# An attention tower with experts on one core: score masks and row maxima cut into 32x32 tiles, and keys, values and value projections laid out in lots of 32 rows

## The reference

```python
Q, K, V = x @ wq, x @ wk, x @ wv            # 16 heads of 16
# local attention: query i sees the keys i-63 .. i
sc = Q_block @ [K_previous_block, K_own_block].T / 4     # 64 queries x 128 keys
sc = where((j > i) & (j <= i + 64) & (first block: j >= 64), sc, -inf)
local = softmax(sc) @ [V_previous_block, V_own_block]
# remote attention: 8 heads over 64 pooled latents, causal mask lmask
rem = softmax(where(lmask, GQ @ GK.T / 4, -inf)) @ GV @ r_out_w
out = (sigmoid(Q.gate_local) * local + sigmoid(Q.gate_remote) * rem) @ w_out
```

## Time and profile before

| what | value |
|---|---|
| median of 3 runs | 3002.09 us (2997.6 to 3002.82) |
| profiled execution | 3003.33 us |
| its span in the trace | 3001.5 us |
| PE matmul busy | 2668.5 us, 89% |
| PE weight loads busy | 1793.9 us, 60% |
| DVE busy | 1795.5 us, 60% |
| ACT busy | 1091.1 us, 36% |
| mean granted PE clock | 0.971 |

### The profile page before, as it was taken

One profiled execution on the slowest core, in us unless ns is written; L12 is line 12 of the kernel. 1 busy time (PEld: TensorE's weight loads), 2 busy tenths in 40 slices (PEclk: granted clock), 3 DMA queues, 4 the chain that ended last, 5 costly groups with the idle time before them and its releaser, 6 DMA issues. The chain is left out here.

```text
span 3001.5 us, 83138 instructions
## 1 busy us (share of the span) xinstructions
PE 2668.5 (89%) x32904; PEld 1793.9 (60%) x32904; DVE 1795.5 (60%) x5503; ACT 1091.1 (36%) x1898; POOL 752.9 (25%) x998
## 2 busy tenths in 40 slices
PE   2899899899999899899899994299999999999998
PEld 1566666666666566566666663166656565666666
DVE  4556556556556556566566556775767667675720
ACT  0343343343343343433333431143333434343343
POOL 1011111121121121121121100134444453434543
PEclk9999999999999999999999998599999999999999
DMA  2000000010010010010000001001020211101020
GB/s 71 11 23 24 17 24 23 17 28 18 17 28 18 18 29 16 19 28 16 21 26 16 23 9 45 15 29 59 30 64 28 65 46 49 64 28 61 30 67 29
DMA packets 51568, 93.71 MB, mean 31 GB/s; under 512 B 7980, under 2 KB 36728, under 8 KB 51096
## 3 DMA queue, kind: packets, MB, share of 16 engines
q0 software_dynamic: 18432, 50.36, 5.9%
q1 hardware_dynamic: 32792, 38.52, 3.9%
HBM read 55.29 MB, written 33.55 MB: 30 GB/s over the span
## 5 line engine op out<-in xcount | busy, mean ns | idle before, releaser
L985 PE MATMUL S_ps<-hT,w 128*128 128x512 f32 x1024 | 478.4, 614 | 15.1 <-ACT hT L694 12.1
L998 PE MATMUL O_ps<-w,hid 128*128 128x256 f32 x2048 | 460.3, 379 | 0.0
L496 POOL DMA_INDIRECT rows<-in_tok_table,idx_now x128 | 129.4, 1011 | 1171.5 <-PE M_ps L883 928.0
L998 PEld LDWEIGHTS O_ps<-w,hid 128*128 128x128 f32 x2048 | 383.0, 190 | 62.5 <-issue 15.3
L1096 DVE TENSOR_REDUCE mxL<-S_ps 128x16 f32<-128x2048 f32 x128 | 293.0, 2289 | 155.8 <-PE S_ps L804 155.8
L632 ACT ACTIVATE PT<-S_ps 128x2048 f32<-128x2048 f32 x128 | 240.3, 1878 | 279.0 <-PE S_ps L772 279.0
L705 ACT ACTIVATE hid<-S_ps,b 128x512 f32<-128x512 f32 x256 | 175.3, 687 | 425.4 <-PE S_ps L985 408.5
L985 PEld LDWEIGHTS S_ps<-hT,w 128*128 128x128 f32 x1024 | 190.0, 194 | 223.5 <-issue 212.1
L828 PEld LDWEIGHTS O_ps<-bdV,PT 128*64 128x64 f32 x7680 | 249.2, 138 | 53.4 <-issue 47.5
L665 ACT ACTIVATE bdV<-M_ps 64x256 f32<-64x256 f32 x256 | 98.8, 386 | 490.7 <-PE M_ps L900 489.2
L828 PE MATMUL O_ps<-bdV,PT 128*64 128x34 f32 x7680 | 263.6, 225 | 1.9 <-DVE loc L1112 1.9
(11 more groups left out here) (237 smaller groups left out, 4248.5 us busy)
## 6 DMA issues: line engine op xcount, KB each, us to landing
h_rows<-h SPq DMA_DIRECT2D x64, 256.0 KB, 2.1
w<-in_w SPq DMA_DIRECT2D x16, 1024.0 KB, 5.9
rows<-in_tok_table,idx_now POOLq DMA_INDIRECT x128, 3.5
out_rows<-orow,idx_cur POOLq DMA_INDIRECT x128, 2.4
PT<-in_tables SPq DMA_DIRECT2D x1, 1024.0 KB
b<-in_b SPq DMA_DIRECT2D x8, 128.0 KB, 4.9
hrow<-h_rows,idx_next POOLq DMA_INDIRECT x64
hrow<-h_rows,idx_cur POOLq DMA_INDIRECT x64
```

The source lines that it names most:

```text
L985: mm = nc.tensor.matmul(S_ps[:, m % 2, 0:GT * P], w1[:, c, m * P:(m + 1) * P], hT[g % 2][:, c, :], start=c == 0, stop=c == KC - 1)
L998: mm = nc.tensor.matmul(O_ps[:, q % 2, 0:D], hid[:, m, q * P:(q + 1) * P], w2[:, m, :], start=m == 0, stop=m == FC - 1)
```

## The change

Everything that was cut at 64 is cut at 32. `pe_masks` issues 16 matmuls in tiles of 32x32 in place of 8 in 64x64; row group n of the array always writes bank n, so the mask tables are stored in as many turned copies as needed (`latm` and `reach` four, `lreach` two, `band` three variants). An S6 item takes 96 keys for every 32 queries in place of 128 for 64: 32 fp32 matmuls of 192 moving columns in tiles of 32x32, in place of 16 of 256 in 32x64; the mask is 384 columns wide, and DVE reduces 1536 columns in place of 2048. `Kt` and `bdV` hold even and odd heads in alternating lots of 32 rows. The item V issues 16 matmuls of 128 columns and 8 of 40 in tiles of 128x32, in place of 8 in 128x64; ACT copies V with 128 partitions and a parity scale (`c_parity`, two columns more) in place of 64 partitions without one. The tables grow from 2048 to 3488 columns.

```diff
+QW = 32
+KW = W + QW
 ...
-    cols = [f(ident), f(parity), f(own), f(i), f(band), f(lat), f(np.roll(lat, W, 0)), f(before), f(lane), f(reach), f(lreach), f(pick)]
+    cols = [f(ident), f(parity), f(own), f(i), f(band), f(turned(lat, NG)), f(before), f(lane), f(turned(reach, NG)), f(turned(lreach, 2)), f(pick)]
 ...
-        Kt = [sba(f"Kt{j}", [P, KC, 1 + NB, 2, W]) for j in range(2)]
+        Kt = [sba(f"Kt{j}", [P, KC, 2 * (1 + NB), 2, QW]) for j in range(2)]
 ...
+                v = bank[:, 0:D].rearrange("p (a q d) -> p a q d", a=2, d=HD)
                 for j in range(2):
-                    v = bank[W * j:W * (j + 1), 0:D + 2 * (GW + E)].rearrange("p (a n) -> p a n", a=2)[:, :, 0:D // 2]
-                    nc.scalar.activation(bdV[par][W * j:W * (j + 1), 2 * k:2 * k + 2, :, j, 0:HD],
-                                         v.rearrange("p a (q d) -> p a q d", d=HD), ACT.Copy)
+                    nc.scalar.activation(bdV[par][:, 2 * k:2 * k + 2, :, j, 0:HD], v, ACT.Copy, scale=c_parity[:, 2 + j:3 + j])
 ...
         def pe_masks(pe, into, mask):
-            for g in range(0, NG, 2):
-                for a, n, rows_ in ((0, g, 0), (1, g, W), (1, g + 1, 0), (0, g + 1, W)):
-                    nc.tensor.matmul(into(S_ps[W * a:W * (a + 1), n, :]), identb[rows_:rows_ + W, rows_:rows_ + W],
-                                     mask(a, rows_), start=True, stop=False)
+            for n in range(NG):
+                own_ = slice(QW * n, QW * (n + 1))
+                for a in range(NG):
+                    nc.tensor.matmul(into(S_ps[QW * a:QW * (a + 1), n, :]), identb[own_, own_], mask(own_, a, (n - a) % NG),
+                                     start=True, stop=False)
 ...
-                        for a in range(2):
-                            x = 2 * t + a
-                            into = S_ps[W * a:W * (a + 1), g, D * c:D * (c + 1)].rearrange("p (j a k) -> p a j k", j=2, a=2)
-                            mm = nc.tensor.matmul(into, Qt[par][32 * g:32 * g + 32, c, W * x:W * (x + 1)],
-                                                  Kt[par][32 * g:32 * g + 32, c, x:x + 2, :, :], start=False, stop=c == KC - 1)
+                        for a in range(NG):
+                            x = NG * t + a
+                            into = S_ps[QW * a:QW * (a + 1), g, 2 * KW * c:2 * KW * (c + 1)].rearrange("p (j a k) -> p j a k", j=2, k=QW)
+                            mm = nc.tensor.matmul(into, Qt[par][32 * g:32 * g + 32, c, QW * x:QW * (x + 1)],
+                                                  Kt[par][32 * g:32 * g + 32, c, x:x + 3, :, :].rearrange("p a j k -> p j a k"),
+                                                  start=False, stop=c == KC - 1)
 ...
-                for n in range(2):
-                    lhs = [x1T[:, c, W * (2 * k + n):W * (2 * k + n + 1)] for c in range(KC)]
-                    to = n * (D // 2 + gates_)
+                lot = lambda c, n: x1T[:, c, P * k + QW * n:P * k + QW * (n + 1)]
+                for n in range(2):
                     for c in range(KC):
-                        for a, (lo, hi) in enumerate((even, odd)):
 ...
+                        for a in range(NG):
+                            mm = nc.tensor.matmul(bank[QW * a:QW * (a + 1), n * (D // 2):(n + 1) * (D // 2)], lot(c, 2 * n + a // 2),
+                                                  wvg[:, c, slice(*halves[a % 2])], start=c == 0, stop=c == KC - 1)
+                for c in range(KC):
+                    for a in range(NG):
+                        mm = nc.tensor.matmul(bank[QW * a:QW * (a + 1), D:D + GW + E], lot(c, a), wvg[:, c, gates_],
+                                              start=c == 0, stop=c == KC - 1)
 ...
-                    nc.vector.tensor_reduce(mxL[:, k - 6, :], S_ps[:, :, :].rearrange("p g (h n) -> p (g h) n", n=P),
+                    nc.vector.tensor_reduce(mxL[:, k - 6, :].rearrange("p (g h) -> p g h", g=NG),
+                                            S_ps[:, :, 0:4 * KW].rearrange("p g (h n) -> p g h n", n=KW),
                                             AX.X, ALU.max, negate=True).then_inc(s_mx, 1)
```

More of the change, by code:

```diff
@@ L58, in constants @@
     ident = np.eye(P, dtype=np.float32)
[L59 to L62, removed]
+    near, wide = i[:, None] % QW, np.arange(KW)[None, :]
+    ring = (wide > near) & (wide <= near + W)
+    band = np.stack([np.where(m, 0.0, NEG) for m in (ring & (wide >= W), ring & (wide >= W - QW), ring)], 1)
     tiles = S // P
@@ L65, in constants @@
     lat = np.where(np.arange(NL)[None, None, :] <= tok // (S // NL), 0.0, NEG)
-    parity = np.stack([(i // HD) % 2 == 0, (i // HD) % 2 == 1], 1)
+    parity = np.stack([(i // n) % 2 == j for n in (HD, QW) for j in range(2)], 1)
     own = (i[:, None] // HD == np.arange(LH)[None, :]) * (NL / S)
@@ L221, in tower @@
         mp = sba("mp", [P, TS, P])
-        reach = sba("reach", [P, 2 * W], BF16)
-        lreach = sba("lreach", [P, S], BF16)
+        reach = sba("reach", [P, NG, 2 * W], BF16)
+        lreach = sba("lreach", [P, 2, S], BF16)
         pick = sba("pick", [P, KC + 1, 2 * W], BF16)
@@ L240, in tower @@
         xf, xw, xs = (stage[0:SEQS, 6144 + S * n:6144 + S * (n + 1)] for n in (1, 2, 3))
[L241 to L242 removed]
+        woutT = stage[:, 3584:3584 + KC * D].rearrange("p (c n) -> p c n", c=KC)
+        ones = stage[:, 6144 + S:6144 + S + P]
         wvs = PL[:, 0, :].rearrange("p (c n) -> p c n", c=KC)
@@ L888, in pe_item @@
             elif name == "V":
-                even, odd, gates_ = (0, D // 2), (D // 2 + GW + E, D + GW + E), GW + E
+                halves, gates_ = ((0, D // 2), (D // 2 + GW + E, D + GW + E)), slice(D // 2, D // 2 + GW + E)
+                lot = lambda c, n: x1T[:, c, P * k + QW * n:P * k + QW * (n + 1)]
                 for n in range(2):
-                    lhs = [x1T[:, c, W * (2 * k + n):W * (2 * k + n + 1)] for c in range(KC)]
-                    to = n * (D // 2 + gates_)
                     for c in range(KC):
-                        for a, (lo, hi) in enumerate((even, odd)):
-                            first = to
-                            if a == n:
-                                lo, hi = (lo, hi + gates_) if a == 0 else (lo - gates_, hi)
-                                first = to if a == 0 else to - gates_
-                            mm = nc.tensor.matmul(bank[W * a:W * (a + 1), first:first + hi - lo], lhs[c], wvg[:, c, lo:hi],
-                                                  start=c == 0, stop=c == KC - 1)
+                        for a in range(NG):
+                            mm = nc.tensor.matmul(bank[QW * a:QW * (a + 1), n * (D // 2):(n + 1) * (D // 2)], lot(c, 2 * n + a // 2),
+                                                  wvg[:, c, slice(*halves[a % 2])], start=c == 0, stop=c == KC - 1)
+                for c in range(KC):
+                    for a in range(NG):
+                        mm = nc.tensor.matmul(bank[QW * a:QW * (a + 1), D:D + GW + E], lot(c, a), wvg[:, c, gates_],
+                                              start=c == 0, stop=c == KC - 1)
             mm.then_inc(s_misc, 1)
@@ L1361, in _ @@
             for par in range(2):
-                nc.vector.memset(Kt[par][:, :, 0, :, :], 0.0)
+                nc.vector.memset(Kt[par][:, :, 0:2, :, :], 0.0)
                 chain(dve, nc.vector.memset(bdV[par][:, :, :, :, :], 0.0))
-                nc.vector.memset(bdV[par][0:W, :, :, 0, HD:OW], 1.0)
-                nc.vector.memset(bdV[par][W:P, :, :, 1, HD:OW], 1.0)
+                for a in range(NG):
+                    nc.vector.memset(bdV[par][QW * a:QW * (a + 1), :, :, a % 2, HD:OW], 1.0)
                 chain(dve, nc.vector.memset(bdL[par][:, :, :, :], 0.0))
```

46 lines of the change are left out of this document (24 added, 22 removed).

## The result

The changed kernel takes 3023.16 us, median of 4 runs (3017.86 to 3026.01), beside 3002.45 us for the kernel before (its profiled execution counted in, four runs): a ratio of 1.0069, 95% interval 1.0049 to 1.0089. It is slower by about 21 us, where 87 us less had been forecast. The profiled execution is the fastest of the four, with a span of 3016.1 us.

The account below looks back on a forecast made before the run. PE was taken to bound the kernel. Per sequence 1.08 + 0.53 + 1.50 - 0.12 - 0.17 = 2.82 us, x 32 = 90.2, less 3.5 of setup, 86.7 us: 2916.6, or 2915.5 as a median; range 2888 to 3002.

Parts of the forecast that it names:

- Bottleneck: Attention stage: PE, busy 89% of the span, sets the time; only S7's mask waits for DVE, 1.16 us each.
- Masks of S0 to S5: Six masks a sequence: 16 tiles at once take 0.38 us in place of 0.56, saving 1.08 us.
- Items S6 to S9: Mask plus scores: 1.10 us in place of 1.60, bounds 1.03 to 1.40; S7 to S9 save 1.50 us a sequence.
- case C: Rival, scores of S6 to S9: only some ten of 16 tiles stay busy, 1.40 us an item, 2944 us; chance 0.20.
- the spread of the starts: Scores of S6 to S9: 16 fp32 starts 7 ns apart fit within a 0.16 us pass, adding 0.10 us.
- The twelve starts in 0.07 us: PE behind the wait ahead of S7: twelve instructions issued in about 0.07 us, taken as evidence that starts are cheap.
- S6: Item S6: PE's saving is hidden by DVE; only the shorter reduction, 1.76 us, counts, saving 0.53 us.
- V: Value projection: same 592 columns in four tile columns side by side; more starts cost 0.12 us a sequence.
- ACT: Copies of V: the parity scale adds 0.087 us to each of two, delaying the transpose by 0.17 us a sequence.
- Setup: Before PE's start: 1440 more table columns, larger casts and four small memsets add 3.5 us.
- something unforeseen: Whole kernel: slower by an uncounted cause, say instruction fetch delivering half as much again in the dense stretch; chance 0.03.
- Case A: Rival, items S6 to S9 and V: feeding limits PE at 25 ns a pair, 3038 us with setup; chance 0.07.

Follow-up runs that it names:

- run 9: The changed kernel with the odd heads' scores left out (96 moving columns in place of 192, same instruction count): 3023.57 us, ratio 1.0074.
- run 3: The kernel before with each score matmul of S6 to S9 cut in two of 128 columns, four pairs in a row for a tile: 3037.14 us, ratio 1.0117.
- run 4: The kernel before with the S6 to S9 score matmuls cut in two, but two pairs in a row for a tile: 3020.61 us, ratio 1.0064.
- run 2: The kernel before with only the value projection changed, to 24 matmuls in 128x32 tiles: 3000.82 us, ratio 0.9997.
- run 5: The changed kernel with scores, their mask and the reduction cut as before (32x64, 256 columns; 2048 reduced): 2954.96 us, ratio 0.9849.
- run 8: The changed kernel with four wide fp32 matmuls (the filler) ahead of the third V item: 3108.88 us; control, masks alone with the same filler: 3069.53 us.
- run 6: Masks and V as in the changed kernel, scores as in run 4, the same count of PE instructions as the changed kernel: 3028.81 us, ratio 1.0086.
- run 7: Masks alone, with each projection of Q and K cut into four of 128 columns, 60 pairs more a sequence: 2965.97 us, ratio 0.9883.
- masks alone: The kernel before with only the masks changed to 16 tiles of 32x32, tables turned likewise: 2955.67 us, ratio 0.985.

## Why the prediction was wrong

Step by step, per sequence, from the means between starts:

- **Bottleneck.** PE's time per item sets the time, and only S7 waits for DVE: right for the kernel before. It does not hold for the kernel after, in which a third thing, the supply of PE's instructions, ends the waits of the dense stretch.
- **Masks of S0 to S5.** 0.368 us for a forecast of 0.38: 6 x 0.19 = 1.14 saved for 1.08. Right. The 10.6 times for 16 tiles that the prediction quotes from the Trainium skill ("TensorE: Matmul & The Clock Gate", Measured speedup vs the span model) stand there without a data type; the runs here compare 16 tiles with four, not with the whole array.
- **Items S6 to S9: the step that failed first.** Forecast 1.10 us, bounds 1.03 to 1.40. Mask and scores take 0.179 + 1.526 = 1.71 us before O and 0.179 + 1.455 = 1.63 before V, more than the 1.60 of before. S7 to S9 were to save 1.50 and cost 0.23. Undisturbed the item is 0.17 + 1.26 = 1.43 us: the size of case C (1.40), which I had at 0.20. The term of the sum that failed is the spread of the starts, 0.10 us, taken from 7 ns a start: pairs start so only as long as instructions stand ready, the first 18 of an item, and 17 ns apart in the mean from there, so that the last starts 1.01 us behind the first (run 9). The twelve starts in 0.07 us were such a burst. I took 1.10 although no row showed more than eight tiles fed. The ground of case C, pairs of one tile behind each other, does cost time (runs 3 and 4), but its price, all streaming divided by ten, would have given 0.75 us in run 9, where 0.94 were measured. The rest, from 1.43 to 1.67 in the mean, is holes.
- **S6.** The reduction measures 1755 ns for 1.76. From S6's mask to S7's it is 0.18 + 1.46 + 3.11 = 4.74 us for 5.01: 0.26 saved where 0.53 was reckoned.
- **V: the second failure.** Four streams work (run 2), but the second pair of V costs 3.31 us for 2.48: +0.83 where -0.06 was due. It is holes, not work: 2.43 to 2.50 us in runs 2, 5 and 8.
- **O, counted nowhere.** +0.28 for the item behind S7's scores, nothing for the one behind S5, +0.52 for the one at the end of a sequence: every other sequence has a hole of 1.0 to 1.4 us there, while the back edge of the loop got 0.9 us shorter.
- **The clock behind the end of a sequence, counted nowhere.** From 366 to 1715 us six stretches of 3.4 us at 1.2 GHz lie in the middle of loop turns, each from within or just behind an O with such a hole; the kernel before has none there. The items of L857 to L870 cost +0.29 us a sequence in the mean. The eight pairs of L857 with a hole ahead but the clock at 1.00, and behind the start of such a stretch:

```profile
255.98 1.09 PE L857 MATMUL M_ps<-cst,xn 128*128 128x128 f32 x8
480.09 1.97 PE L857 MATMUL M_ps<-cst,xn 128*128 128x128 f32 x8
```

From the start of O to the next mask such a sequence takes 7.98 us (475.8 us) where one with a hole alone takes 6.36 (252.5), 0.3 of it for the longer hole: about 1.3 us, six times, 8 of the 21 us by this estimate. They come behind holes, but not every kernel with holes has them: the trace of run 6 has no such stretch.

- **ACT.** The copies grew by 98 ns each for 87. The wait of the transpose got shorter, not longer (2.6 us from 300 to 1900 us, 7.0 before), since a hole of PE mostly lies ahead of it.
- **Setup.** PE starts 4.05 us later for 3.5. Right. (The casts of tables grew by 1440 columns, 1792 to 3232, not from 1280 to 2824; the 0.8 us stay.)

In sum -1.14 + 0.23 - 0.26 + 0.83 + 0.28 + 0.52 + 0.29 = +0.75 us a sequence, 23 us for the 30 sequences measured. The first sequence is 4.7 us shorter and the setup 4 longer: 22 us, where the first matmul of the next stage comes 22.8 us later and the medians differ by 21. (What follows, which the change does not touch, happens to be 8 us shorter in this profile, so that the two spans differ by 14.6 only.)

The prediction said that PE's instructions grow "by 40% or so" and counted that at nothing; instruction fetch stood as an example of something unforeseen, inside 0.03. This was the wrong price: 80 packets more came in the same stretch, and they were countable beforehand, one for each 256 instructions. In the dense stretch PE could execute a block in 3.0 to 3.1 us, while two packets there never start less than about 3.3 us apart, so holes were bound to come once the stretch was long enough. The Trainium skill ("Runtime: NRT & Kernel Launch", Instruction fetch mechanics) says that instructions come in blocks of 16 KiB, 256 of them, fetched while the one before is executed, and that crossing a boundary is mostly hidden. The trace agrees on the block (254 and 250 between holes) and not on the cost: it is hidden in the kernel before and costs up to 1.2 us a block here. Case A (feeding at 25 ns a pair) comes nearest to the time, 3038, by another mechanism: 127 pairs in 4.1 us are 32 ns a pair through the dense stretch, but only once what was fetched ahead is used up. That the holes are a wait for fetched blocks is shown by their fixed places, whole blocks apart and moved with the code in run 8, by the landings ahead of them and by runs 5 to 8 together; no record names it outright, and how much PE holds ahead was not measured. Nor does the rate of a transfer look like the limit: at the back edges two packets start 1.1 to 1.4 us apart. It looks as if the next block is asked for too late; that was not tested.

## What to carry to other kernels

Before cutting matmuls smaller, count PE's instructions through the densest stretch as one counts bytes: some 256 in 4 us is what was sustained here, and a good part of what is saved in or ahead of such a stretch can come back as waits. Take the part of a change that lowers time for few instructions more (the masks, 80 pairs a sequence, 45 us less), leave the part that doubles the count of the densest items (the scores, 128 pairs), and put few long matmuls, not many short ones, where the density is highest. A burst of starts measured after a wait says how fast waiting instructions go off, not what can be fed for long: here 7 ns a pair at first and 17 later.

## What the runs showed of the hardware

- Sixteen bf16 tiles of 32x32 run fully side by side: 16 matmuls of 512 columns in 0.368 us, where 8 in 64x64 took 0.558.
- Starts of fp32 pairs are 3 to 7 ns apart at the head of an item, but 16 to 17 ns apart for most of the rest of 64 pairs in 32x32 (run 9), and through much of S5 in masks alone (1.34 us for 1.10 at the same columns, cause open).
- A wait for instructions shows as idle PE with "issue" in brackets, at places that leave the same number when divided by 256: 206 or 207 in after and in run 6, 171 or 172 in after with filler.
- Two pairs or four in a row for one tile, all else equal, made 1.137 or 1.455 us of the same 64 pairs.
- The granted clock of after drops for a moment in the middle of a loop turn as well, not only around the back edge: 0.68 from 705 to 709 us in the row below, where the kernel before had 1.00. Before it fell, from 700 to 704 us, PE was busy for 2.90 of 4 us, with a hole of 1.1 us in O. The columns are those of the earlier trace rows.

```profile
700.00:704.00 4.00, 2.90 (x125) 2.47 (x108) 2.68 (x5) 0.62 (x4) 0.00 (x0) 1.00 0.02 4
705.00:709.00 4.00, 4.00 (x35) 3.13 (x33) 1.83 (x6) 1.79 (x3) 0.00 (x0) 0.68 0.00 0
```
